# Linear attention: the queries' features as the stationary operand, denominators as a 65th column, the result turned for the output product

## The chip, the cores and the metric

One Trainium2 chip, one of its cores. The metric is the device time of one execution in microseconds (us), the median of several. A core has TensorE (PE; its weight loads are listed as PEld), VectorE (DVE), ScalarE (ACT), GpSimd (POOL) and SyncE (SP), which runs the DMA queue used here. The engines run side by side and order their work by semaphores.

## The reference

Eight sublayers in a row, each added to x (16 batches of 112 rows of 256). The change is in the third, a linear attention of x to a context of 375 rows:

```python
B, L, HID, H, DH, M = (4, 1024, 256, 16, 64, 128)
def _relu_kernel(x, proj):
    ratio = 1.0 / float(np.sqrt(proj.shape[0]))
    return jax.nn.relu(ratio * jnp.einsum('blhd,md->blhm', x, proj)) + EPS
q = jnp.einsum('bld,dhk->blhk', query_input, Wq)
k = jnp.einsum('bld,dhk->blhk', source_input, Wk)
v = jnp.einsum('bld,dhk->blhk', source_input, Wv)
qp = _relu_kernel(q, proj)
kp = _relu_kernel(k, proj)
kvs = jnp.einsum('blhm,blhd->bhmd', kp, v)
num = jnp.einsum('blhm,bhmd->blhd', qp, kvs)
ks_sum = jnp.sum(kp, axis=1)
den = jnp.einsum('blhm,bhm->blh', qp, ks_sum)
att = num / den[..., None]
return jnp.einsum('blhd,hdk->blk', att, Wo)
```

So 16 heads of 64 values, each with 128 features per row.

## The kernel before

The sublayer is `linear_attention_phase`. Most products are made from 16-bit parts: an operand is split into a high half (`HI`, ScalarE as a rule) and a low half (`LO`, VectorE or GpSimd), and a product is the sum of three (`PARTS`).

All engines walk through the same list of steps, 16 to a batch (`SLOTS`), written out by hand in `units_at`. Within a batch, t counts its steps. In steps 0 to 7 a key product is made per step (`k`); the features of the keys (`features`) are made in steps 5, 7, 9, 10, 12 and 14, the values (`v`) in steps 8, 9, 11, 12, 13 and 15. Every second batch also makes the queries of two batches: `q` in the odd steps, their features (`qf`) in steps 6, 10, 14 and 18. A batch then goes on under the steps of the next one: the sums over the context in steps 18 to 21 (`sums`, 36 products of 65 columns each; the 65th column of the values is one, so it holds the sum of the features), then `den`, `ratio` and `out`. Step 16 + n of a batch is step n of the next, and within a step the older batch comes first.

Each engine takes the units of a step in that order, and its queue is strict:

- TensorE makes the products. Those of `k`, `v`, `q`, `features` and `qf` go to five PSUM banks in a ring (`p_bank`); before a bank is written, TensorE waits until the unit that held it has been taken (`claim`, `taken`). Three banks hold the sums (`kvs_bank`), the numerators and the output (`num_bank`) and the broadcast denominators (`den_bank`).
- ScalarE makes the high parts: those of keys, queries and values from PSUM; those of the features one step later, from `kp` (`high_features`).
- VectorE makes the low parts of keys, queries and values, and takes the features from PSUM (ReLU and the small constant) to `kp`, which has four places.
- GpSimd makes the low parts of the features (`low_features`, L1260), two instructions per unit, and those of the divided result (`low_att`, L1266), and splits the next context in step 4.

The quotient before: in step 22 `denominators` (L1566) multiplies the queries' features with the sums of the features, FP32, 16 products into four groups of 32 rows. VectorE (`invert`) takes the reciprocal and splits it in three bfloat16 parts. In steps 25 and 28 `ratio` makes the numerators of eight heads, transposed (64 values x 112 rows, FP32, two heads at a time), and spreads the reciprocals over the rows with 12 bfloat16 products against a selector. ScalarE copies the numerators (`take_num`), VectorE multiplies (`divide`), ScalarE and GpSimd split the result (`high_att`, `low_att`, steps 27 and 30). In step 35 `out_product` (L1596) makes 24 products, and VectorE adds the result to X in step 36.

The context of a batch comes by DMA from SyncE, once GpSimd's split has emptied the buffer.

Of the kernel before, what the change touches and what calls it, by code (L numbers as in the profile page):

```python
# [17 lines left out]
H = 16  # L18
# [1096 lines left out]
def linear_attention_phase(nc, tag, X, XT, ident, ctxT, Wq, Wk, projT, Wv, Wo):  # L1115
# [50 lines left out]
    with ExitStack() as st:  # L1166
# [10 lines left out]
        qp = qp_flat[:, :].rearrange("p (g r c s) -> p g r c s", g=2, r=2, c=C)  # L1177
# [9 lines left out]
        summed, kvs_evac, den_done, inverted, divided, att_done, out_done, x_done = (  # L1187
            m.sem(n) for n in ("summed", "kvs_evac", "den_done", "inverted", "divided", "att_done", "out_done", "x_done"))
        dks_blank, sel_made, num_taken = m.sem("dks_blank"), m.sem("sel_made"), m.sem("num_taken")
        wo_hi, wo_split, att_hi, att_split, part, rden_split = (  # L1190
            m.sem(n) for n in ("wo_hi", "wo_split", "att_hi", "att_split", "part", "rden_split"))
# [38 lines left out]
        kvs = m.sb("kvs", [128, H, VC])  # L1230
        dks = m.sb("dks", [128, H, 32])
        sel = m.sb("sel", [128, C, 128], BF16)
        rden = m.sb("rden", [128, 3, S])
        rden16 = m.sb("rden16", [128, 3, S], BF16)
        wo16 = m.sb("wo16", [128, 2, C, D], F16)
        att16 = m.sb("att16", [128, 2, C, S], F16)
        attT = m.sb("attT", [128, C, S])
        p_bank = [m.bank(f"p{i}") for i in range(RING)]
        kvs_bank, num_bank, den_bank = m.bank("kvs_sum"), m.bank("num"), m.bank("den")

        with nc.Block() as block:
# [7 lines left out]
            def _(pool):  # L1249
# [14 lines left out]
                def low_att(b, hf):  # L1264
                    pool.wait_ge(att_hi, 2 * b + hf + 1)
                    pool.tensor_tensor(att16[:, LO, 4 * hf:4 * hf + 4, :], attT[:, 4 * hf:4 * hf + 4, :],  # L1266
                                       att16[:, HI, 4 * hf:4 * hf + 4, :], ALU.subtract).then_inc(att_split, 1)

                split_context(0)
                pool.memset(dks[:, :, :], 0.0).then_inc(dks_blank, 1)  # L1270
                pool.memset(v16[:, HI, :, :, DH:VC], 1.0).then_inc(ones_made, 1)
                pool.memset(v16[:, LO, :, :, DH:VC], 0.0).then_inc(ones_made, 1)
                for h in range(H):
                    row = 32 * (h % 4) + 8 * (h // 4)
                    pool.tensor_copy(sel[:, h // 2, h % 2 * DH:(h % 2 + 1) * DH],
                                     ident[:, row:row + 1].to_broadcast([128, DH])).then_inc(sel_made, 1)
                for s in steps:
                    for unit in units_at(s):
                        if unit[0] == "features":
                            low_features(unit)  # L1280
                    if s % SLOTS == 4 and s // SLOTS + 1 < B:
                        split_context(s // SLOTS + 1)
                    for b in range(B):
                        if s - SLOTS * b in (27, 30):
                            low_att(b, (s - SLOTS * b - 27) // 3)

            @block.scalar
            def _(act):
# [11 lines left out]
                def evacuate(unit):  # L1300
# [19 lines left out]
                    elif kind == "sums":  # L1320
                        act.wait_ge(summed, 4 * b + c + 1)
                        if b >= 1:
                            act.wait_ge(divided, 2 * b)
                        act.copy(kvs[:, 4 * c:4 * c + 4, :],
                                 src[:, 0:4 * VC].rearrange("p (h d) -> p h d", d=VC)).then_inc(kvs_evac, 1)
                        if b == c == 0:
                            act.wait_ge(dks_blank, 1)
                        if b >= 1:
                            act.wait_ge(den_done, b)
                        act.copy(dks[:, 4 * c:4 * c + 4, 8 * c:8 * c + 8],  # L1330
                                 src[:, 0:4 * VC].rearrange("p (h d) -> p h d", d=VC)[:, :, DH:VC].to_broadcast([128, 4, 8])
                                 ).then_inc(kvs_evac, 1)

                def take_num(b, hf):
                    act.wait_ge(divided, 2 * b + hf + 1)
                    if b >= 1:
                        act.wait_ge(out_done, b)
                    act.copy(attT[:, 4 * hf:4 * hf + 4, :].rearrange("p n s -> p (n s)"), num_bank[:, 0:4 * S]).then_inc(num_taken, 1)

                def high_att(b, hf):  # L1340
                    act.wait_ge(att_done, 2 * b + hf + 1)
                    act.copy(att16[:, HI, 4 * hf:4 * hf + 4, :], attT[:, 4 * hf:4 * hf + 4, :]).then_inc(att_hi, 1)
# [17 lines left out]
                for s in steps:  # L1360
                    if s >= 1:
                        for unit in units_at(s - 1):
                            if unit[0] == "features":
                                high_features(unit)
                    for unit in units_at(s):
                        if unit[0] in ("k", "q", "v", "sums"):
                            evacuate(unit)
                        elif unit[0] == "ratio":
                            take_num(unit[1], unit[2])
# [3 lines left out]
                    for b in range(B):  # L1373
                        if s - SLOTS * b in (27, 30):
                            high_att(b, (s - SLOTS * b - 27) // 3)
# [6 lines left out]
            def _(dve):  # L1382
# [5 lines left out]
                def take(unit):  # L1388
                    kind, b, c = unit
                    bank = place[unit][0]  # L1390
                    src = p_bank[bank]
# [23 lines left out]
                    elif kind == "qf":  # L1415
                        dve.wait_ge(projected["qf"], qfeats[unit] + 1)
                        if b >= 2:
                            dve.wait_ge(divided, 4 * b - 4)
                        for r, bank in enumerate(place[unit]):
                            dve.tensor_scalar(qp[:, b % 2, r, 2 * c:2 * c + 2, :],  # L1420
                                              p_bank[bank][:, 0:2 * QW].rearrange("p (c s) -> p c s", s=QW), 0.0, EPS * WS,
                                              ALU.max, ALU.add).then_inc(qp_done, 1)

                def invert(b):
                    dve.wait_ge(den_done, b + 1)
                    if b >= 1:
                        dve.wait_ge(divided, 2 * b)
                        dve.wait_ge(rden_split, b)
                    dve.reciprocal(rden[:, 0, :], kvs_bank[:, 384:384 + S]).then_inc(inverted, 1)
                    dve.wait_ge(inverted, b + 1)  # L1430
                    for i in range(2):
                        dve.tensor_copy(rden16[:, i, :], rden[:, i, :]).then_inc(part, 1)
                        dve.wait_ge(part, 4 * b + 2 * i + 1)
                        dve.tensor_tensor(rden[:, i + 1, :], rden[:, i, :], rden16[:, i, :], ALU.subtract).then_inc(part, 1)
                        dve.wait_ge(part, 4 * b + 2 * i + 2)
                    dve.tensor_copy(rden16[:, 2, :], rden[:, 2, :]).then_inc(rden_split, 1)

                def divide(b, hf):
                    half = attT[:, 4 * hf:4 * hf + 4, :].rearrange("p n s -> p (n s)")
                    dve.wait_ge(num_taken, 2 * b + hf + 1)  # L1440
                    dve.tensor_tensor(half, den_bank[:, 0:4 * S], half, ALU.mult).then_inc(att_done, 1)
# [5 lines left out]

                dve.wait_ge(wk_hi, 1)
# [1401 lines left out]
```

## Time and profile before

| | |
|---|---|
| time, median of 3 runs | 2585.32 us (2584.45 to 2588.91) |
| the profiled execution | 2593.29 us, of which span 2591.3 us |
| PE busy over the span | 2213.3 us (85%), 23986 products |
| DVE, ACT, POOL busy | 1561.2, 1411.5, 953.2 us |
| mean granted clock of TensorE | 0.92 of full speed |

The phase of the change runs from about 518 us to 1125 us of the span. The time is the median; the rows come from the one profiled execution. In the rows, `a_kp` is a feature tile, `a_p` the ring of banks, `a_kvs_sum`, `a_num` and `a_den` the three other banks; "128*112" behind a product is rows x columns of its stationary operand, followed by the moving one.

### The profile page before, as it was taken

The numbers are of one execution on the slowest core, as the hardware profiler recorded it, in microseconds if no ns is written. First come the engines' busy times: TensorE is split into PE (matmuls) and PEld (weight loads), VectorE is DVE, ScalarE is ACT, GpSimd is POOL, SyncE is SP. The second block draws the span as 40 slices with busy tenths as digits, with TensorE's granted clock in tenths as the row PEclk, the third lists the DMA queues.
The fourth block names the chain that finished last, engine by engine and source line by source line (L and its number), as shares of the span: only waits on it lengthen the run. The fifth ranks groups of instructions, "written<-read, shape, count | busy, mean of one in ns | idle before, by whom it ended". The sixth has DMA issues, their size and how long they took to land. (4 is left out here: it accounts for less than half of the span.)

```text
span 2591.3 us, 62717 instructions
## 1 busy us (share of the span) xinstructions
PE 2213.3 (85%) x23986; PEld 1467.9 (57%) x23986; DVE 1561.2 (60%) x3640; ACT 1411.5 (54%) x2999; POOL 953.2 (37%) x1066
## 2 busy tenths in 40 slices
PE   5889399599999999968699999999974993899755
PEld 2556255367777777745456666666652541566533
DVE  3667572476566556636767777777756544556463
ACT  3666563365555555425466666666663542566543
POOL 3443222154444444404423333333322632433043
PEclk8999699799999999969899999999986995999978
DMA  6563361300000000010200000000023214333133
GB/s 129 111 116 71 111 216 38 119 20 14 14 14 8 14 14 2 2 33 1 87 14 9 15 14 9 15 14 9 2 85 103 67 56 124 87 79 73 26 114 109
DMA packets 118581, 139.59 MB, mean 54 GB/s; under 512 B 15072, under 2 KB 107184, under 8 KB 118288
## 3 DMA queue, kind: packets, MB, share of 16 engines
q1 hardware_dynamic: 110900, 115.39, 17.3%
q0 software_dynamic: 7392, 20.19, 2.5%
q8 instruction: 200, 3.28, 0.5%
q14 instruction: 89, 0.73, 0.1%
HBM read 93.25 MB, written 17.47 MB: 43 GB/s over the span
## 5 line engine op out<-in xcount | busy, mean ns | idle before, releaser
L952 DVE TENSOR_REDUCE a_mx<-a_pair 112x2 f32<-112x750 f32 x256 | 238.0, 936 | 194.9 <-PE a_pair L1021 194.9
L1260 POOL TENSOR_TENSOR a_kp<-a_kp 125x512 f16<-125x512 f32 x192 | 217.6, 1158 | 259.1 <-ACT a_kp L1351 259.1
L353 POOL TENSOR_SCALAR a_P<-a_P,a_inv 112x375 f32<-112x375 f32 x256 | 148.4, 593 | 378.5 <-DVE a_inv L484 377.4
L890 ACT ACTIVATE a_PT<-a_pair 125x672 f32<-125x672 f32 x256 | 186.2, 730 | 71.1 <-PE a_pair L1033 66.3
L391 ACT ACTIVATE a_P<-a_masked,a_least 112x375 f32<-112x375 f32 x256 | 153.5, 600 | 83.5 <-DVE a_least L479 81.6
L1394 DVE SCALAR_TENSOR_TENSOR a_k<-a_p,a_k 128x375 f16<-128x375 f32 x128 | 69.3, 547 | 138.7 <-ACT a_k L1307 138.7
L1351 ACT CAST a_kp<-a_kp 125x512 f16<-125x512 f32 x192 | 110.4, 617 | 76.4 <-DVE a_kp L1413 76.4
L572 PE MATMUL a_p<-a_kc,a_wk 128*128 128x375 f16 x768 | 147.1, 327 | 4.3 <-POOL a_kc L347 4.3
L1493 PE MATMUL a_p<-a_kc,a_wk 128*128 128x375 f16 x768 | 142.4, 327 | 6.3 <-POOL a_kc L1252 6.3
L586 PE MATMUL a_p<-a_wv,a_kc 128*125 128x512 f16 x576 | 141.9, 383 | 5.2 <-DVE a_v L518 3.6
L479 DVE CUSTOM_DVE_ANT_0 a_masked<-a_s,a_mask_add 112x375 f32<-112x375 f32 x256 | 129.9, 545 | 27.1 <-PE a_s L609 26.1
L1493 PE MATMUL a_p<-a_wv,a_kc 128*125 128x512 f16 x576 | 141.0, 385 | 0.0
L2522 ACT ACTIVATE all_XT<-f_hb 128x512 f32<-128x512 f32 (+1 forms) x98 | 53.2, 549 | 152.6 <-PE f_hb L2434 136.2
L2434 PE MATMUL f_hb<-w_w1h,f_x 128*128 x588 | 134.9, 367 | 0.0
L1413 DVE TENSOR_SCALAR a_kp<-a_p 125x512 f32<-125x512 f32 x192 | 122.8, 681 | 8.2 <-PE a_p L1524 8.2
L509 DVE SCALAR_TENSOR_TENSOR a_k<-a_p,a_k 128x375 f16<-128x375 f32 x128 | 70.2, 549 | 82.9 <-ACT a_k L402 82.9
L619 PE MATMUL a_t<-all_ident,a_P 112*125 112x112 f32 x768 | 116.6, 288 | 3.4 <-POOL a_P L353 3.4
L489 DVE TENSOR_TENSOR a_PT<-a_t,a_PT 125x336 f16<-125x336 f32 x256 | 116.8, 498 | 1.5 <-ACT a_PT L427 1.5
L619 PEld LDWEIGHTS a_t<-all_ident,a_P 112*125 112x125 f32 x768 | 93.9, 188 | 38.8 <-issue 34.6
L1033 PE MATMUL a_pair<-a_q,a_k 50*125 50x112 f16 (+1 forms) x1536 | 89.5, 224 | 20.7 <-DMA a_q<-a_mT 13.8
L1052 PE MATMUL a_y<-a_PT,a_values 125*32 125x112 f32 x3072 | 102.7, 268 | 5.1 <-ACT a_PT L890 4.9
L586 PEld LDWEIGHTS a_p<-a_wv,a_kc 128*125 128x125 f16 x576 | 77.8, 137 | 49.7 <-DVE a_k L509 6.8
(446 smaller groups left out, 5324.1 us busy)
## 6 DMA issues: line engine op xcount, KB each, us to landing
a_kc<-in_ctxT SPq DMA_DIRECT2D x64, 375.0 KB, 4.0
a_k<-a_k_parts SPq DMA_DIRECT2D x192, 93.8 KB
w_stage<-in_L_ffn_W SPq DMA_DIRECT2D x32, 512.0 KB
w_stage<-in_L_ffn_ew SPq DMA_DIRECT2D x16, 512.0 KB, 6.9
w_stage<-expert_rows SPq DMA_DIRECT2D x16, 448.0 KB, 8.0
a_v_in_sb<-in_ctx SPq DMA_DIRECT2D x16, 375.0 KB
a_q<-a_q_parts SPq DMA_DIRECT2D x48, 112.0 KB, 3.6
w_stage<-in_L_ffn_W SPq DMA_DIRECT2D x16, 256.0 KB, 3.9
```

The source lines that it names most:

```text
L353: pool.tensor_scalar(P[:, p % 4, r, :], P[:, p % 4, r, :], inv[:, p % 4, r:r + 1], 1.0, ALU.mult, ALU.mult).then_inc(P_done, 1)
L391: act.activation(P[:, p % 4, r, :], masked[:, p % 2, r, :], ACT.Exp, bias=least[:, p % 4, r:r + 1], scale=-1.0, accum_out=total[:, p % 4, ...
L479: dve.tensor_tensor_reduce(masked[:, p % 2, r, :], s_bank[0:S, r, 0:SK], mask_add[:, b % 2, :], 1.0, 3e38, ALU.add, ALU.min, least[:, p % ...
L572: mm = pe.matmul(out[:, 0:SK], wk16[:, z, j, c * 128:(c + 1) * 128], kc16[:, b % 2, x, j, :], start=i == j == 0, stop=(i, j) == (2, DC - 1))
L586: mm = pe.matmul(out[0:KP, 0:512], kc16[:, b % 2, x, j, jk * KP:(jk + 1) * KP], wv16[:, z, j, w * 512:(w + 1) * 512], start=i == j == 0, s ...
L619: mm = pe.transpose(t_bank[0:KP, r, j * S:(j + 1) * S], P[:, p % 4, r, j * KP:(j + 1) * KP], ident[0:S, 0:S])
L890: act.activation(PT[:, p % 4, :, :], pair_bank[slot["turned", p]][0:KP, :, 0:KT * S], ACT.Exp).then_inc(exp_done, 1)
L952: dve.tensor_reduce(mx[:, b % 2, 2 * pair:2 * pair + 2], pair_bank[slot["score", p]][0:S, :, 0:SK], AX.X, ALU.max).then_inc(max_done, 1)
L1260: pool.tensor_tensor(kp16[:, LO, j, hf, r, :, :].rearrange("p c m -> p (c m)"), kp[:, n % 4, :], kp16[:, HI, j, hf, r, :, :].rearrange("p ...
L1413: dve.tensor_scalar(kp[:, n % 4, :], p_bank[bank][0:KP, 0:512], 0.0, EPS * WS, ALU.max, ALU.add).then_inc(f_evac, 1)
L1493: mm = pe.matmul(out, lhs(x, z, j), rhs(x, z, j), start=i == j == 0, stop=(i, j) == (2, DC - 1))
L2434: mm = pe.matmul(bank[:, 0:BW], x16[:, j % 2, x, c, :], w.w1h[:, z, c, bass.ds(e, 1), cols].rearrange("p o f -> p (o f)"), start=False, st ...
```

## The change

The quotient is made the other way round, with the rows of x on the partitions.

- The queries' features are now split in 16-bit parts: VectorE writes them to `qpf` (four places), ScalarE makes the high part one step later (`high_queries`), GpSimd the low part (`low_queries`).
- The sums are split too: ScalarE makes the high part from `kvs_bank`, and VectorE the low part from the same bank after it; TensorE's next sums wait for the latter.
- `denominators`, the reciprocal's parts, the selector and the broadcast are gone. `weigh` in steps 23 and 25 makes, per head, three products with the features of 112 rows as stationary operand and the 65 columns of the head's sums moving: seven heads, then nine. Column 65 is the denominator of each row.
- VectorE divides (`divide`, steps 24 and 26) per row with a reciprocal per head. ScalarE and GpSimd split the result, in steps 26 and 28 (before 27 and 30).
- `turn` in step 31 transposes both parts, eight products each; the high part waits for ScalarE's two halves, the low part for GpSimd's two. ScalarE copies the turned high part (`take_high`) and VectorE the low one (`take_low`) for the output product, which stays in step 35.

```diff
-            found += [("den", b, 0)] if t == 22 else []
-            found += [("ratio", b, 0)] if t == 25 else [("ratio", b, 1)] if t == 28 else []
+            found += [("num", b, 0)] if t == 23 else [("num", b, 1)] if t == 25 else []
+            found += [("turn", b, 0)] if t == 31 else []
...
+        pieces = [[(first_bank, 0, 0, 7)], [(num_bank, 0, 7, 14), (kvs_bank, 4 * VC, 14, 16)]]
+        halves = (slice(0, 7), slice(7, H))
...
+                def low_queries(unit):
+                    _, g, c = unit
+                    for r in range(2):
+                        n = 2 * qfeats[unit] + r
+                        pool.wait_ge(qp_hi, n + 1)
+                        pool.tensor_tensor(qp16[:, g % 2, LO, r, 2 * c:2 * c + 2, :],
+                                           qpf[:, n % 4, :].rearrange("p (c s) -> p c s", s=QW),
+                                           qp16[:, g % 2, HI, r, 2 * c:2 * c + 2, :], ALU.subtract).then_inc(qp_low, 1)
+
+                def low_att(b, i):
+                    pool.wait_ge(att_hi, 2 * b + i + 1)
+                    pool.tensor_tensor(atr16[:, LO, halves[i], :], att[:, halves[i], :], atr16[:, HI, halves[i], :],
+                                       ALU.subtract).then_inc(att_split, 1)
...
-                for h in range(H):
-                    row = 32 * (h % 4) + 8 * (h // 4)
-                    pool.tensor_copy(sel[:, h // 2, h % 2 * DH:(h % 2 + 1) * DH],
-                                     ident[:, row:row + 1].to_broadcast([128, DH])).then_inc(sel_made, 1)
                 for s in steps:
                     for unit in units_at(s):
                         if unit[0] == "features":
                             low_features(unit)
+                        elif unit[0] == "qf":
+                            low_queries(unit)
                     if s % SLOTS == 4 and s // SLOTS + 1 < B:
                         split_context(s // SLOTS + 1)
                     for b in range(B):
-                        if s - SLOTS * b in (27, 30):
-                            low_att(b, (s - SLOTS * b - 27) // 3)
+                        if s - SLOTS * b in (26, 28):
+                            low_att(b, (s - SLOTS * b - 26) // 2)
...
+                        act.mul(kvs16[:, HI, 4 * c:4 * c + 4, :], src[:, 0:4 * VC].rearrange("p (h d) -> p h d", d=VC),
+                                1.0 / WS).then_inc(kvs_hi, 1)
...
+                def take_high(b):
+                    act.wait_ge(att_turned, 2 * b + 1)
+                    if b >= 1:
+                        act.wait_ge(out_done, b)
+                    act.copy(att16[:, HI, :, :].rearrange("p c s -> p (c s)"),
+                             first_bank[:, :].bitcast(F16)[:, 0:C * S]).then_inc(high_taken, 1)
+
+                def high_queries(unit):
+                    _, g, c = unit
+                    if g >= 2:
+                        act.wait_ge(weighed, 4 * g - 4)
+                    for r in range(2):
+                        n = 2 * qfeats[unit] + r
+                        act.wait_ge(qp_done, n + 1)
+                        act.copy(qp16[:, g % 2, HI, r, 2 * c:2 * c + 2, :],
+                                 qpf[:, n % 4, :].rearrange("p (c s) -> p c s", s=QW)).then_inc(qp_hi, 1)
...
+                    else:
+                        dve.wait_ge(kvs_hi, 4 * b + c + 1)
+                        dve.scalar_tensor_tensor(kvs16[:, LO, 4 * c:4 * c + 4, :],
+                                                 kvs_bank[:, 0:4 * VC].rearrange("p (h d) -> p h d", d=VC), 1.0 / WS,
+                                                 kvs16[:, HI, 4 * c:4 * c + 4, :], ALU.mult, ALU.subtract).then_inc(kvs_done, 1)
+
+                def divide(b, i):
+                    dve.wait_ge(weighed, 2 * b + i + 1)
                     if b >= 1:
...
+                        dve.wait_ge(att_split, 2 * b)
+                    for piece in pieces[i]:
+                        h0, h1 = piece[2:]
+                        dve.reciprocal(rden[:, h0:h1].unsqueeze(2), weights_of(*piece)[:, :, DH:VC]).then_inc(inverted, 1)
+                    for n, piece in enumerate(pieces[i]):
+                        h0, h1 = piece[2:]
+                        dve.wait_ge(inverted, 3 * b + i + n + 1)
+                        ins = dve.tensor_tensor(att[:, h0:h1, :], weights_of(*piece)[:, :, 0:DH],
+                                                rden[:, h0:h1].unsqueeze(2).to_broadcast([S, h1 - h0, DH]), ALU.mult)
+                    ins.then_inc(att_done, 1)
...
-                        pe.wait_ge(kvs_evac, 8 * b + 2 * g)
+                        pe.wait_ge(kvs_done, 4 * b + g)
...
+                def weigh(b, i):
                     g, t = divmod(b, QB)
...
+                    pe.wait_ge(kvs_done, 4 * b + 2 * i + 2)
+                    pe.wait_ge(qp_low, 8 * (g + 1))
+                    if b >= 1 and i == 0:
+                        pe.wait_ge(high_taken, b)
+                    elif b >= 1:
                         pe.wait_ge(x_done, b)
...
+                    for piece in pieces[i]:
+                        bank, at, h0, h1 = piece
+                        for h in range(h0, h1):
+                            for n, (x, z) in enumerate(PARTS):
+                                mm = pe.matmul(bank[0:S, at + (h - h0) * VC:at + (h - h0 + 1) * VC],
+                                               qp16[:, g % 2, x, h % 2, h // 2, t * S:(t + 1) * S], kvs16[:, z, h, :],
+                                               start=n == 0, stop=n == 2)
+                    mm.then_inc(weighed, 1)
+
+                def turn(b):
+                    if b == 0:
+                        pe.wait_ge(ready16, 1)
+                    for x, bank, made in ((HI, first_bank, att_hi), (LO, num_bank, att_split)):
+                        pe.wait_ge(made, 2 * b + 2)
+                        for c in range(C):
+                            mm = pe.transpose(bank[:, :].bitcast(F16)[:, c * S:(c + 1) * S],
+                                              atr16[:, x, 2 * c:2 * c + 2, :].rearrange("s h d -> s (h d)"), ident16[:, :])
+                        mm.then_inc(att_turned, 1)
+
                 def out_product(b):
-                    pe.wait_ge(att_split, 2 * b + 2)
+                    pe.wait_ge(high_taken, b + 1)
+                    pe.wait_ge(low_taken, b + 1)
```

## Rows read from the trace of the kernel before

**Rows 1.** Windows, 35 us of the phase: busy us per engine, granted clock, DMA, GB/s.

```profile
878.00:913.00 35.00, 34.67 (x508) 26.50 (x506) 22.05 (x44) 18.03 (x41) 14.51 (x13) 1.00 0.04 13
```

**Rows 2.** Timeline of PE, batch without queries: start, length, engine, line, product, count.

```profile
847.64 1.26 PE L1554 MATMUL a_kvs_sum<-a_v,a_kp 125*128 125x65 f16 x36
848.73 1.13 PE L1493 MATMUL a_p<-a_kc,a_wk 128*128 128x375 f16 x6
849.70 1.25 PE L1554 MATMUL a_kvs_sum<-a_v,a_kp 125*128 125x65 f16 x36
...
854.73 0.97 PE L1566 MATMUL a_kvs_sum<-a_qp,a_dks 128*32 128x112 f32 x32
855.64 2.10 PE L1493 MATMUL a_p<-a_kc,a_wk 128*128 128x375 f16 x12
...
860.08 0.99 PE L1582 MATMUL a_num<-a_qp,a_kvs 128*64 128x112 f32 x16
861.00 0.76 PE L1586 MATMUL a_den<-a_rden,a_sel 128*128 128x112 bf16 x12
861.70 0.91 PE L1524 MATMUL a_p<-a_pp,a_k 64*125 64x128 f16 x24
862.53 1.51 PE L1493 MATMUL a_p<-a_wv,a_kc 128*125 128x512 f16 x6
...
872.27 1.51 PE L1493 MATMUL a_p<-a_wv,a_kc 128*125 128x512 f16 x6
```

**Rows 3.** Timeline of PE in another sublayer, 112 stationary columns, 120 to 8 moving.

```profile
305.32 1.52 PE L2482 MATMUL f_o<-f_hot,r_ones 112*112 112x120 f16 x15
306.70 0.23 PE L2484 MATMUL f_o<-f_heads,r_ones 112*112 112x8 f16 x1
```

**Rows 4.** Windows over those products (columns as in rows 1).

```profile
305.00:310.00 5.00, 1.74 (x17) 1.68 (x17) 4.66 (x15) 2.99 (x5) 0.00 (x0) 0.50 0.40 125
```

**Rows 5.** Groups by line, 518 to 1130 us: count, busy us, mean ns, idle before.

```profile
L1260 POOL TENSOR_TENSOR a_kp<-a_kp 125x512 f16<-125x512 f32 x192 | 217.6, 1158 | 259.1 <-ACT a_kp L1351 259.1
...
L1266 POOL TENSOR_TENSOR a_att<-a_attT,a_att 128x448 f16<-128x448 f32 x32 | 33.1, 1036 | 21.2 <-ACT a_att L1342 21.2
...
L1324 ACT COPY a_kvs<-a_kvs_sum 128x260 f32<-128x260 f32 x64 | 24.0, 375 | 72.2 <-PE a_kvs_sum L1554 72.2
...
L1441 DVE TENSOR_TENSOR a_attT<-a_den,a_attT 128x448 f32<-128x448 f32 x32 | 19.7, 615 | 7.2 <-ACT a_attT L1338 7.2
```

**Rows 6.** Timeline of POOL, low parts of steps 9 and 10, both kinds of batch.

```profile
828.10 4.51 POOL L1260 TENSOR_TENSOR a_kp<-a_kp 125x512 f16<-125x512 f32 x4 [1.59 <-ACT a_kp L1351]
...
865.26 4.51 POOL L1260 TENSOR_TENSOR a_kp<-a_kp 125x512 f16<-125x512 f32 x4 [1.12 <-ACT a_kp L1351]
```

**Rows 7.** Timeline of PE, values of steps 9 and 15, batch with queries.

```profile
825.04 1.51 PE L1493 MATMUL a_p<-a_wv,a_kc 128*125 128x512 f16 x6
...
838.33 1.51 PE L1493 MATMUL a_p<-a_wv,a_kc 128*125 128x512 f16 x6
```

**Rows 8.** Timeline of the phase's end, with idle time before in brackets.

```profile
1091.57 1.51 PE L1493 MATMUL a_p<-a_wv,a_kc 128*125 128x512 f16 x6
...
1097.08 4.33 PE L1596 MATMUL a_num<-a_wo,a_att 128*112 128x256 f16 x24 [2.92 <-POOL a_att L1266]
...
1103.15 1.25 PE L1554 MATMUL a_kvs_sum<-a_v,a_kp 125*128 125x65 f16 x36 [0.65 <-ACT a_dks L1330]
...
1124.84 0.42 DVE L1445 SCALAR_TENSOR_TENSOR all_X<-a_num,all_X 112x256 f32<-112x256 f32 x1 [6.29 <-PE a_num L1596]
```

**Rows 9.** Windows of 1 us: the clock comes back (columns as in rows 1).

```profile
144.00:145.00 1.00, 1.00 (x22) 0.69 (x14) 0.77 (x3) 0.39 (x1) 0.00 (x0) 0.76 1.08 159
...
1100.00:1101.00 1.00, 1.00 (x10) 1.00 (x9) 0.00 (x0) 0.00 (x0) 0.00 (x0) 0.90 0.00 0
```

**Rows 10.** Timeline of PE, a group of six after idle times in another sublayer.

```profile
80.64 0.38 PE L1033 MATMUL a_pair<-a_q,a_k 50*125 50x112 f16 x6 [2.09 <-DMA a_q<-a_mT]
...
139.15 0.57 PE L1033 MATMUL a_pair<-a_q,a_k 50*125 50x112 f16 x6 [3.25 <-DMA a_q<-a_mT]
```

More of the change, by code:

```diff
@@ L1322, in evacuate @@
                         if b >= 1:
[L1323 to L1332, printed above, removed]
@@ L1389, in take @@
                     kind, b, c = unit
-                    bank = place[unit][0]
-                    src = p_bank[bank]
+                    src = kvs_bank if kind == "sums" else p_bank[place[unit][0]]
                     if kind == "k":
@@ L1424, in invert @@
-                def invert(b):
-                    dve.wait_ge(den_done, b + 1)
-                    if b >= 1:
[L1427 to L1441, printed above, removed]
+                            n = 2 * qfeats[unit] + r
+                            if n >= 4:
+                                dve.wait_ge(qp_low, n - 3)
+                            dve.tensor_scalar(qpf[:, n % 4, :], p_bank[bank][:, 0:2 * QW], 0.0, EPS * WS, ALU.max,
+                                              ALU.add).then_inc(qp_done, 1)
+                    else:
[3 more added lines that the diff above has]
+                                                 kvs16[:, HI, 4 * c:4 * c + 4, :], ALU.mult, ALU.subtract).then_inc(kvs_done, 1)
@@ L1462, in _ @@
                     for unit in units_at(s):
-                        if unit[0] in ("k", "q", "v", "features", "qf"):
+                        if unit[0] in ("k", "q", "v", "features", "qf", "sums"):
                             take(unit)
@@ L1557, in sums @@
                     mm.then_inc(summed, 1)
-                def denominators(b):
+                def weigh(b, i):
                     g, t = divmod(b, QB)
-                    pe.wait_ge(kvs_evac, 8 * b + 8)
-                    taken(pe, ("qf", g, 3), 1)
-                    for i in range(H // 4):
-                        for a in range(4):
-                            h = 4 * i + a
-                            mm = pe.matmul(kvs_bank[32 * a:32 * a + 32, 384:384 + S], dks[:, h, :],
-                                           qp[:, g % 2, h % 2, h // 2, t * S:(t + 1) * S], start=i == 0, stop=i == H // 4 - 1)
-                    mm.then_inc(den_done, 1)
@@ L1604, in _ @@
                             sums(unit[1], unit[2])
-                        elif unit[0] == "den":
-                            denominators(unit[1])
-                        elif unit[0] == "ratio":
-                            ratio(unit[1], unit[2])
+                        elif unit[0] == "num":
+                            weigh(unit[1], unit[2])
+                        elif unit[0] == "turn":
+                            turn(unit[1])
                         elif unit[0] == "out":
```

94 lines of the change are left out of this document (38 added, 56 removed).

## The prediction

> **What bounds the kernel now.** I read the 35 us windows of the phase first. The reader is to see that TensorE is busy for all but a third of a microsecond at full clock, while VectorE, ScalarE and GpSimd are busy for 22, 18 and 15 us [rows 1]. So in the linear attention (518 to 1125 us of the span) a microsecond taken from TensorE's queue is a microsecond of the kernel, and each wait of TensorE that is added costs its whole length. Second, the timeline of TensorE gives the price of each group from start to start [rows 2, 7]. Third, GpSimd's timeline and groups show how far behind TensorE the low parts come [rows 5, 6]. Last, the end of the phase and the clock after idle stretches [rows 8 to 10].
>
> **TensorE's work per batch.** Removed: denominators, 854.73 to 855.64 = 0.91 us, and twice a ratio, 860.08 to 861.70 = 1.62 us [rows 2]; together 4.15 us. Added: 16 heads x 3 = 48 products, with 112 columns stationary and 65 moving, and 16 turning products. No row shows 112x65. The sums (128 stationary, 65 moving) take 847.64 to 848.73 for 36, 30 ns each [rows 2]. The nearest row with 112 stationary columns has 15 products with 120 down to 8 moving columns, in 305.32 to 306.70, 92 ns each [rows 3], at a granted clock of 0.50 [rows 4]; their moving columns average 64, which at 1.2 GHz would be 53 ns, while 112 columns are 93 ns: the stationary part sets their pace, and at full clock that is 46 ns. Bounds for the 48: 1.45 us and 2.2 us. I take 2.2, since that row has this number of stationary columns.
>
> The Trainium skill (TensorE: Matmul & The Clock Gate, section Weight-path perf modes) says that the fast weight load is on only when the number of weights is 128 and the type is not FP32. By that rule the 112 columns load slowly, as the row at half clock has it, and the sum is 2.2 us; if they loaded as the sums' 128 do it would be 1.45.
>
> The turning products have 128 stationary and 112 moving 16-bit columns, like the 12 broadcasts at 861.00 to 861.70, 58 ns each [rows 2]: 16 x 58 ns = 0.93 us, 0.46 for either part. TensorE saves 4.15 - 2.2 - 0.93 = 1.0 us per batch (1.8 by the other bound).
>
> **The wait that is added.** The turning product of batch b stands in step 31, which is step 15 of the next batch, and needs GpSimd's second low part of the divided rows. GpSimd issues that in step 28 (step 12 of the next batch) behind the low parts of the features of steps 9, 10 and 12 and behind its own first half; in batches with queries also behind two low parts of query features (step 10). Before, the output product of step 35 was what waited for it, four steps later. Worked out from the end of the features of step 9, which is the start of the values' product of step 9:
> - Batch without queries. TensorE: 862.53 to 872.27 = 9.74 us, less the second ratio that has moved or gone, 1.62, plus the high half of the turning, 0.46: it wants the low part at 8.6 us [rows 2]. GpSimd: starts 865.26, that is 2.7 us in, 4.5 us for four feature parts [rows 6], 1.04 for 448 elements, 2.3 for two feature parts, and for 576 elements (by the step from 448 to 512) 1.3 [rows 5]: 11.9 us. TensorE waits 3.3 us.
> - Batch with queries. TensorE: 825.04 to 838.33 = 13.3, less 1.62 plus 0.46 = 12.1 us [rows 7]. GpSimd: starts 828.10, so 3.1 + 4.5 + two query parts of 448 elements, 2.1, + 1.0 + 2.3 + 1.3 = 14.3 us [rows 5, 6]. It waits 2.1 us, part of it perhaps sooner, where the query product of step 14 claims a bank.
>
> Behind the waiting turn stand the values' product of step 15 and then everything; nothing else on TensorE can go ahead, so the wait is lost. The turns fall in batches 1 to 15, of which 8 are without queries and 7 with: 8 x (3.3 - 1.0) + 7 x (2.1 - 1.0) = 26 us more.
>
> **The clock.** After 3.25 us without a product TensorE went on at half clock [rows 10], until 144.5, 5.3 us later (0.76 in that microsecond [rows 9]); after 2.92 us [rows 8] until 1100.2, 3.1 us later [rows 9]. After 2.09 us a group of six still took 0.38 us, not 0.57 [rows 10]. So I expect the 3.3 us waits to cost the clock and the 2.1 us waits not to. TensorE's queue is full after them, so half of the slow stretch is lost: 1.6 to 2.6, say 2.1 us, x 8 = 17 us.
>
> **Sums.** The next sums waited for ScalarE alone (copy 0.375 us [rows 5], done just before one key product had passed). Now VectorE reads the same bank after it; 260 elements by the 0.615 us for 448 [rows 5] are about 0.42 us. Sums end + 0.2 + 0.38 + 0.05 + 0.42 = 1.05 to 1.1 us against the key product's 0.97 (848.73 to 849.70): 0.1 us, some 1.5 times per batch, 3 us in all.
>
> **Costed at nothing.** VectorE loses the inversion and its five small operations and gains four low parts of the sums, three small reciprocals and the 896-element copy; ScalarE gains four query parts per batch and loses eight small copies. Each gains 1 to 1.5 us per batch beside 13 and 17 us idle [rows 1]. If that cover were gone it would be TensorE's banks that come back late, at most those 1.5 us per batch, 24 us. GpSimd's sixteen selector copies at the start go too; nothing waits for them before the first ratio. The small copy of the identity ahead of VectorE's first split adds 0.2 us. No transfer is added or moved: the context's loads still wait for GpSimd's split in step 4.
>
> **The end.** Before: from the last values' product to the last add 1091.57 to 1125.26, 33.7 us [rows 8]. There the output product waited 2.92 us for GpSimd, then ran at half clock; the chain of the inversion and two halves, one after the other, followed. After, counted from the same product (estimates from the rows above): values and the copies out of the turn 3.8; output product 2.6 at full clock; three sums, now 2.2 apart instead of 1.25 + 0.65 = 1.9 [rows 8], 5.5; weighing 2.5; dividing 1.4; high part 0.7; low part 1.3; low turn at half clock and its copy 2.0; output 4.5 and add 0.4: 25 us. That gives back 9 us.
>
> **Sum.** +26 + 17 + 3 + 0.2 - 9 = +37 us. On the profiled execution, 2591.3 us of span and 2.0 around it, that makes 2630. That execution stood 0.3% above the median of the runs; on the median, 2585.3, it makes 2622.
>
> **Rivals.**
> - *The wait without the clock.* For it: the waits could come out a few tenths shorter, and one gap of 2.09 us left the clock alone. Against it: gaps of 2.92 and 3.25 us both lost it. +20 us: 2605.
> - *No wait at all: faster.* GpSimd's low part would have to be ready 3.3 us sooner relative to TensorE, for instance if its parts of features came 1 us each rather than 1.16 and ScalarE's high parts sooner. Then 16 x 1.0 us and the 9 us of the end come in, less 3 for the sums: -22 us, 2563; with 30 ns for a weighing product, -12 more. It decides where the wait falls under 1.0 us in a batch. Against it: its busy time and start are rows, and between features 9 and the turn GpSimd has no idle time to give.
> - *A wait of half the size,* since TensorE's earlier arrival at the features lets ScalarE and GpSimd begin sooner: about 1.2 us per batch. 15 x (1.2 - 1.0) + 3 - 9 = -3 us, within 0.2%: 2582.
> - *More waits.* The 2.1 us waits lose the clock too (7 x 2.1 = 15 us), or ScalarE's extra parts delay the features: 2637, at most 2660.
> - *The change does less than it says:* were 16-bit weighing as dear as FP32, TensorE would save nothing: 16 us on the forecast, 2638.
>
> **Chances.** Forecast 0.46, wait without the clock 0.20, half wait 0.08, faster 0.14, the two dear ones 0.12. Range: left out are the faster case and most of what lies above 2650, so 2590 to 2650. The slower cases' own range is 2600 to 2650. Within 0.2% (5 us, about what a measurement of this kernel can tell from no change): 0.08; faster 0.14; slower 0.78.
>
> **What the profile after would show.** Right: a row of idle time before the low half of the turning product, released by GpSimd's low part of the divided rows, about 3 us in batches without queries and 2 in the others; granted clock under 1.00 in the windows of the batches without queries; weighing products 46 ns apart; about 1 us less matmul work per batch at full clock; the last output product some 9 us closer to the last values. Wrong: GpSimd idle ahead of that low part, windows at 1.00 throughout, or waits of TensorE elsewhere (banks, sums). The likeliest ways to be wrong are the length of the wait, a difference of two long sums, and how long the clock stays down.

## The result, and the profile after

The changed kernel takes 2624.49 us (median of 4 runs, 2622.21 to 2634.08), the kernel before, run beside it, 2585.91. The ratio is 1.0155, 95% interval 1.0127 to 1.0182: slower by about 1.5%, 38.6 us between the medians. The forecast was 2622, that is +37.

The profiled execution of the changed kernel is the longest of its four, 2634.08 us, and some 6 us of that lie ahead of the phase: its first key product starts at 524.31 us, against 518.13 before. So I measure the phase by itself, from that product to the end of the last add. Before: 518.13 to 1125.26, 607.1 us. After: 524.31 to 1169.92, 645.6 us, 38.5 more. That is as much as the medians differ by. The agreement is closer than it can be relied on: a second execution of the changed kernel, below, has a phase of 640.8 us, and the phase before is known from one execution only, which lies 8 us above its median.

Windows over the same 35 us of the span as [rows 1], changed kernel (length, then busy us of PE, PEld, DVE, ACT, POOL with counts, granted clock, DMA share, GB/s):

```profile
878.00:913.00 35.00, 31.82 (x428) 23.35 (x423) 19.18 (x38) 17.27 (x35) 19.31 (x17) 0.95 0.05 13
```

TensorE was busy for 34.67 us at full clock in [rows 1]; now 3.2 us are empty, the clock is down for a part, and 80 products fewer are done. GpSimd has gained 4.8 us of work. The timeline of TensorE shows the place, first a batch without queries, then one with queries, then the sums (start, length, engine, line, product, count; in brackets idle time and its releaser):

```profile
826.73 0.57 PE L1609 MATMUL a_first<-a_ident,a_atr 112*128 112x112 f16 x8
830.36 0.93 PE L1609 MATMUL a_num<-a_ident,a_atr 112*128 112x112 f16 x8 [3.06 <-POOL a_atr L1281]
...
868.01 0.91 PE L1551 MATMUL a_p<-a_pp,a_k 64*125 64x128 f16 x24
869.77 0.75 PE L1561 MATMUL a_p<-a_q,a_pp 64*128 64x224 f16 x12 [0.85 <-DVE a_v L1422]
870.45 0.57 PE L1609 MATMUL a_first<-a_ident,a_atr 112*128 112x112 f16 x8
872.26 0.57 PE L1609 MATMUL a_num<-a_ident,a_atr 112*128 112x112 f16 x8 [1.24 <-POOL a_atr L1281]
872.66 1.47 PE L1520 MATMUL a_p<-a_wv,a_kc 128*125 128x512 f16 x6
...
1120.79 1.13 PE L1520 MATMUL a_p<-a_kc,a_wk 128*128 128x375 f16 x6
1121.98 1.25 PE L1581 MATMUL a_kvs_sum<-a_v,a_kp 125*128 125x65 f16 x36
```

The low half of the turn waits for GpSimd's low part in every one of the 15 batches that turn beside a following one: about 3.05 us in the 8 without queries, 1.24 us in the 7 with queries. In those 7 the query product of step 14 also waits 0.85 us for its bank (0.28 us in the kernel before). The sums that have only a key product ahead of them start 1.19 us after it, where [rows 2] have 0.97; there are three such places in two batches.

The bank wait grew from 0.28 to 0.85 us because of ScalarE's queue. Here is ScalarE, first in the changed kernel, then in the kernel before:

```profile
866.24 0.60 ACT L1330 ACTIVATE a_v<-a_p 125x512 f16<-125x512 f32 x1 [1.28 <-PE a_p L1520]
866.74 0.66 ACT L1343 CAST a_atr<-a_att 112x576 f16<-112x576 f32 x1
867.30 1.14 ACT L1369 CAST a_kp<-a_kp 125x512 f16<-125x512 f32 x2
868.34 0.60 ACT L1330 ACTIVATE a_v<-a_p 125x512 f16<-125x512 f32 x1
```

```profile
835.19 1.13 ACT L1351 CAST a_kp<-a_kp 125x512 f16<-125x512 f32 x2
836.22 0.60 ACT L1318 ACTIVATE a_v<-a_p 125x512 f16<-125x512 f32 x1
...
836.95 0.57 ACT L1342 CAST a_att<-a_attT 128x448 f16<-128x448 f32 x1
```

The second high part of the divided rows moved from step 30 to step 28. It now stands ahead of the features and of the values' high part, where it stood behind them. Counted from TensorE's values' product of steps 12 and 13 (864.70 now, 833.15 before), the values' high part starts after 3.64 us instead of 3.07. VectorE's low part, which gives the bank back, comes after it. These 0.57 us are the growth of the wait; the piece was not moved back to try it.

The weighing products, in the timeline of the batch that begins at 800.85:

```profile
811.99 1.23 PE L1598 MATMUL a_first<-a_kvs,a_qp 128*112 128x65 f16 x21
813.05 1.13 PE L1520 MATMUL a_p<-a_kc,a_wk 128*128 128x375 f16 x6
...
816.29 1.23 PE L1598 MATMUL a_num<-a_kvs,a_qp 128*112 128x65 f16 x21
817.36 0.48 PE L1598 MATMUL a_kvs_sum<-a_kvs,a_qp 128*112 128x65 f16 x6
817.77 0.91 PE L1551 MATMUL a_p<-a_pp,a_k 64*125 64x128 f16 x24
```

21 products take 811.99 to 813.05 = 1.06 us, 50.5 ns each; both groups together 1.06 + 1.48 = 2.54 us per batch. A half of the turn takes 872.26 to 872.66, 0.40 us, 50 ns for each of 8.

The clock after one of the long waits, in windows of 1 us (columns as above):

```profile
829.00:830.00 1.00, 0.00 (x0) 0.00 (x0) 0.31 (x1) 0.96 (x2) 1.00 (x2) 1.00 0.00 0
830.00:831.00 1.00, 0.65 (x8) 0.65 (x9) 0.00 (x0) 0.00 (x0) 1.00 (x2) 0.56 0.00 0
831.00:832.00 1.00, 1.00 (x7) 0.61 (x5) 0.00 (x0) 0.00 (x0) 1.00 (x2) 0.50 0.00 0
832.00:833.00 1.00, 1.00 (x4) 0.61 (x3) 0.00 (x0) 0.00 (x0) 0.52 (x1) 0.50 0.00 0
833.00:834.00 1.00, 1.00 (x6) 0.45 (x5) 0.00 (x0) 0.20 (x1) 0.00 (x0) 0.73 0.00 0
834.00:835.00 1.00, 1.00 (x8) 0.61 (x7) 0.57 (x1) 1.00 (x2) 0.00 (x0) 1.00 0.00 0
```

In this turn the granted clock is still 1.00 for most of the idle time, falls to 0.50 (1.2 GHz of 2.4) in the last quarter of a microsecond before the low half starts, and stays there for 0.44 x 2 + 2 + 0.27 x 2 = 3.4 us. In other turns the fall comes later, up to 1.0 us after the low half has started (the first, at 590.17). Between 560 us and the tail such stretches sum to 37.5 us, as much as eleven of 3.4 us: one at each of the 8 long waits, of which that at 670 us lasts 6.8, and one each near 632 and 714 us, at turns that had waited 1.24 us. The kernel before has none there before 1096 us.

This fall costs about 1.5 us: the low half of the turn takes 0.72 us (830.36 to 831.08) and not 0.40, the values' product behind it 2.52 us (831.08 to 833.60) and not 1.34.

GpSimd's timeline in the last batch, and its groups by line and shape over the phase (count, busy us, mean ns, idle before):

```profile
1135.27 4.50 POOL L1266 TENSOR_TENSOR a_kp<-a_kp 125x512 f16<-125x512 f32 x4 [2.40 <-ACT a_kp L1369]
1139.73 1.04 POOL L1281 TENSOR_TENSOR a_atr<-a_att,a_atr 112x448 f16<-112x448 f32 x1
1140.73 2.27 POOL L1266 TENSOR_TENSOR a_kp<-a_kp 125x512 f16<-125x512 f32 x2
1142.95 1.28 POOL L1281 TENSOR_TENSOR a_atr<-a_att,a_atr 112x576 f16<-112x576 f32 x1
```

```profile
L1275 POOL TENSOR_TENSOR a_qp<-a_qpf,a_qp 128x448 f16<-128x448 f32 x64 | 66.0, 1052 | 41.1 <-ACT a_qp L1359 41.1
...
L1444 DVE SCALAR_TENSOR_TENSOR a_kvs<-a_kvs_sum,a_kvs 128x260 f16<-128x260 f32 x64 | 27.4, 428 | 72.4 <-ACT a_kvs L1336 72.2
L1336 ACT ACTIVATE a_kvs<-a_kvs_sum 128x260 f16<-128x260 f32 x64 | 24.8, 387 | 68.3 <-PE a_kvs_sum L1581 68.3
```

GpSimd has no idle time between the low parts of step 9 and the one that TensorE waits for: 1144.23 - 1135.27 = 8.96 us in one piece. The 64 new query parts add 66 us to its phase.

The tail, in the timeline of all engines, answers to [rows 8]:

```profile
1144.29 0.93 PE L1609 MATMUL a_num<-a_ident,a_atr 112*128 112x112 f16 x8 [3.05 <-POOL a_atr L1281]
...
1145.01 2.73 PE L1520 MATMUL a_p<-a_wv,a_kc 128*125 128x512 f16 x6
...
1154.70 1.25 PE L1581 MATMUL a_kvs_sum<-a_v,a_kp 125*128 125x65 f16 x36 [1.03 <-DVE a_kvs L1444]
...
1165.35 4.11 PE L1620 MATMUL a_num<-a_wo,a_att 128*112 128x256 f16 x24 [0.81 <-DVE a_att L1466]
...
1169.50 0.42 DVE L1471 SCALAR_TENSOR_TENSOR all_X<-a_num,all_X 112x256 f32<-112x256 f32 x1 [4.30 <-PE a_num L1620]
```

From the last values' product to the last add it is now 24.9 us, where [rows 8] have 33.7.

### The profile page after: what moved, and what is told of

It is laid out like the page before. It is cut to its first block and busy times, and to the rows that moved or that the text cites. A ratio compares the mean times of both kernels' runs of the same rounds, so it can differ in the third digit from the quotient of the medians.

```text
span 2632.4 us, 62104 instructions
## 1 busy us (share of the span) xinstructions
PE 2226.3 (85%) x23602; PEld 1477.7 (56%) x23602; DVE 1575.7 (60%) x3689; ACT 1438.1 (55%) x2983; POOL 1014.8 (39%) x1113
## 5 line engine op out<-in xcount | busy, mean ns | idle before, releaser
L1520 PE MATMUL a_p<-a_wv,a_kc 128*125 128x512 f16 x576 | 152.5, 409 | 0.0
L586 PE MATMUL a_p<-a_wv,a_kc 128*125 128x512 f16 x576 | 141.9, 383 | 5.2 <-DVE a_v L518 3.6
L1422 DVE SCALAR_TENSOR_TENSOR a_v<-a_p,a_v 125x512 f16<-125x512 f32 x96 | 66.5, 693 | 112.4 <-ACT a_v L1330 112.4
L1330 ACT ACTIVATE a_v<-a_p 125x512 f16<-125x512 f32 x96 | 57.3, 597 | 101.4 <-PE a_p L1520 101.4
```

The costliest lines, as they stand in the source:

```text
L586: mm = pe.matmul(out[0:KP, 0:512], kc16[:, b % 2, x, j, jk * KP:(jk + 1) * KP], wv16[:, z, j, w * 512:(w + 1) * 512], start=i == j == 0, s ...
L1520: mm = pe.matmul(out, lhs(x, z, j), rhs(x, z, j), start=i == j == 0, stop=(i, j) == (2, DC - 1))
```

## The experiments

Theory: the loss is the turn's place in TensorE's queue, ahead of GpSimd's low part, and the clock that goes with the wait; the arithmetic itself is cheaper. Rivals: the clock alone, or the slow 112-column weighing, or the sums' new wait carries it. The kernels ran on two other chips, with the kernel before beside each set: its median was 2582.85 us for the first four (19 runs) and 2596.41 us for the second four (9 runs). So ratios are compared, and phases of profiled executions, each measured as above. The phases are of one execution each, and no execution of the kernel before was profiled on these two chips.

**Turn two steps later.** The turn and the two copies that take it move from step 31 to step 33:

```diff
-            found += [("turn", b, 0)] if t == 31 else []
+            found += [("turn", b, 0)] if t == 33 else []
```

(and the same number in ScalarE's and VectorE's lists). 

> The changed kernel, with the turning product and its two copies moved from step 31 to step 33; nothing else. Theory (the turning product waits for GpSimd's second low part, and the clock falls after the long waits): both waits (8 x 3.15 us and 7 x 1.4 us, 35 us in all) and the clock's loss (17 us) go, 2624.5 - 52 = about 2572 us, granted clock 1.00 through the phase, faster than the kernel before. Rival A (the wait only moves on, to the output product of step 35, which needs the copies): 2600 or more, with an idle stretch before the output product. Rival B (the time is lost in banks that VectorE and ScalarE give back late under their extra work): 2615 to 2625, the waits of TensorE for VectorE grown.

Measured: 2582.01 us, ratio 0.9999 (0.9985 to 1.0014); phase 599.8 us. Timeline of TensorE, batch without queries:

```profile
727.54 0.56 PE L1609 MATMUL a_first<-a_ident,a_atr 112*128 112x112 f16 x8
728.86 0.57 PE L1609 MATMUL a_num<-a_ident,a_atr 112*128 112x112 f16 x8 [0.76 <-POOL a_atr L1281]
```

The whole loss is gone, and the clock is at full until the tail (behind the phase's first microseconds, which are at half clock in every profile). But I had expected 10 us less. The wait did not vanish in the batches without queries, it is 0.77 us (1.72 in the last of them); and two batches, from output product to output product, take 73.26 us, as in the kernel before (73.10). What the products save there, the rest of this wait, the bank wait of step 14 and the sums use up. In the profiled execution only the shorter end is left as a gain (7.3 us of phase). That execution is 6 us below this kernel's own median; the median gains 0.8 us, and where the other 6 go is not settled. It had the highest mean granted clock of the ten executions (0.921; the median is 0.916, and the slowest, 2588.49 us, had 0.912), so the clock may be where they go, in a part of the kernel that no kept trace shows.

**Low part first on GpSimd.** The turn stays; GpSimd makes the second low part in step 27, ahead of the features of step 12:

```diff
-                        if s - SLOTS * b in (26, 28):
-                            low_att(b, (s - SLOTS * b - 26) // 2)
+                        if s - SLOTS * b in (26, 27):
+                            low_att(b, s - SLOTS * b - 26)
```

> The changed kernel, with GpSimd's second low part of the divided rows issued at the end of step 27, so ahead of the low parts of the features of step 12 instead of behind them; the turning product stays in step 31. Theory (GpSimd's queue makes the part late): the wait shrinks by the two feature parts, 2.3 us: 3.15 to 0.9 us in batches without queries, 1.4 to 0 in the others, and with 0.9 us the clock stays up: 2624.5 - 28 - 17 = about 2579 us. Rival (the part is late because VectorE's division and ScalarE's high part are, and the place in GpSimd's queue is no matter): the wait stays near 3 us, 2624 us.

Measured: 2578.50 us, ratio 0.9982 (0.9967 to 0.9997); phase 601.0 us. TensorE in a batch without queries:

```profile
728.01 0.57 PE L1609 MATMUL a_first<-a_ident,a_atr 112*128 112x112 f16 x8
729.40 0.57 PE L1609 MATMUL a_num<-a_ident,a_atr 112*128 112x112 f16 x8 [0.82 <-POOL a_atr L1281]
```

3.05 became 0.82 us, as two feature parts of 1.16 us less would have it; in batches with queries the wait is gone. So where one instruction stands in the queue of GpSimd, which is idle for 16 of 35 us, decides between 1.0155 and 0.9982.

**The same wait, filled.** TensorE repeats the high half of the turn while it waits, 8 times in batches without queries and 4 times in the others; the repeats write the same values again:

```diff
-                        for c in range(C):
+                        again = (8 if b % 2 == 0 else 4) if x == HI and b < B - 1 else 1
+                        for c in list(range(C)) * again:
```

> The changed kernel, but TensorE repeats the eight products that turn the high part while it would wait: 8 times over in batches without queries, 4 times in the others (8 products take 0.41 us), into the same place. The added products compute nothing new. Theory (the wait itself is 35 us, the clock's fall after it is a further cost of about 17 us): idle stretches of 0.3 and 0.2 us are left, the granted clock stays at 1.00, and the time falls by 14 to 18 us, to about 2609 us. Rival (half clock costs nothing here, since what follows waits for others anyway, or the clock falls in spite of the fill): 2624 us or a little more.

Measured: 2605.86 us, ratio 1.0095 (1.0073 to 1.0117); phase 630.2 us. TensorE:

```profile
738.62 3.32 PE L1610 MATMUL a_first<-a_ident,a_atr 112*128 112x112 f16 x64
742.25 0.57 PE L1610 MATMUL a_num<-a_ident,a_atr 112*128 112x112 f16 x8 [0.31 <-POOL a_atr L1281]
742.65 1.47 PE L1520 MATMUL a_p<-a_wv,a_kc 128*125 128x512 f16 x6
```

The turn ends as late as ever, TensorE only stays busy. The clock is at full until the tail, and the phase is 15.4 us shorter than the changed kernel's; the ratio says 0.6%, 16 us. This is the price of the clock by itself. It is known roughly: against the second execution of the changed kernel, below, the phase is 10.6 us shorter, but the ratio 0.7% lower, 18 us. The rival that the clock alone made the change slow falls too: 1.0095 is left, which is the wait.

**128 stationary columns.** The query features of each batch are stored 128 apart instead of 112, the 16 added columns zero, and the weighing products use all 128:

```diff
-                                mm = pe.matmul(bank[0:S, at + (h - h0) * VC:at + (h - h0 + 1) * VC],
-                                               qp16[:, g % 2, x, h % 2, h // 2, t * S:(t + 1) * S], kvs16[:, z, h, :],
+                                mm = pe.matmul(bank[:, at + (h - h0) * VC:at + (h - h0 + 1) * VC],
+                                               qp16[:, g % 2, x, h % 2, h // 2, t, :], kvs16[:, z, h, :],
```

> The changed kernel, but the queries' features are stored 128 columns apart with 16 blank columns behind each batch's 112, and the weighing products take all 128 as stationary operand (their 16 extra result rows are not read). Theory (the 112 stationary columns set the pace of 51 to 53 ns for 65 moving columns, 128 load faster): 30 ns a product as in the sums, 48 x 21 ns = 1.0 us per batch, 16 us in all: about 2608 us. Rival (the pace is set by the moving part and the issue of the instructions): 50 ns a product as before, 2624 us.

Measured: 2613.17 us, ratio 1.0121 (1.0099 to 1.0144); phase 634.5 us. TensorE:

```profile
720.13 0.81 PE L1604 MATMUL a_first<-a_kvs,a_qp 128*128 128x65 f16 x21
720.77 1.12 PE L1524 MATMUL a_p<-a_kc,a_wk 128*128 128x375 f16 x6
```

More columns are faster: 21 products in 0.64 us, 30.5 ns each against 50.5; 1.57 us per batch against 2.54, so 15.5 us in 16 batches. The Trainium skill (TensorE: Matmul & The Clock Gate, section Weight-path perf modes) has fast weight load on only for 128 weights that are not FP32; by that rule the trace agrees. The edit also moves the places of the features in memory; that and the number of columns were not tried apart. With 1.0121 left, the slow weighing is not what made the change slow. Only 11 us of the 15.5 show in the phase. The clock accounts for most of the rest: half-clock stretches sum to 44.4 us up to the tail instead of 37.5, at 7 of the 8 long waits and now at 5 of the 7 short ones; 6.9 / 2 = 3.4 us of work lost, as an estimate. Two turns of this one execution, both of batches with queries:

```profile
776.09 0.75 PE L1565 MATMUL a_p<-a_q,a_pp 64*128 64x224 f16 x12 [0.85 <-DVE a_v L1426]
...
778.56 0.57 PE L1615 MATMUL a_num<-a_ident,a_atr 112*128 112x112 f16 x8 [1.23 <-POOL a_atr L1282]
778.97 2.73 PE L1524 MATMUL a_p<-a_wv,a_kc 128*125 128x512 f16 x6
...
854.38 0.75 PE L1565 MATMUL a_p<-a_q,a_pp 64*128 64x224 f16 x12 [0.85 <-DVE a_v L1426]
...
856.86 0.57 PE L1615 MATMUL a_num<-a_ident,a_atr 112*128 112x112 f16 x8 [1.23 <-POOL a_atr L1282]
857.27 1.47 PE L1524 MATMUL a_p<-a_wv,a_kc 128*125 128x512 f16 x6
```

The waits are the same, 0.85 and 1.23 us, and the values' product after them takes 2.73 us once and 1.47 us the other time.

**The changed kernel again,** on the second chip, as the measure for the next three. 

> The changed kernel once more, unaltered, beside the kernel before on the chip of the runs it is sent with: 1.5% slower again (1.013 to 1.018), the phase 38 us longer. It is there to be compared with.

Measured: 2638.39 us, ratio 1.0165 (1.0149 to 1.0181); phase 640.8 us. The clock fell 8 times up to the tail, after the long waits alone. So the two further falls of the first profile and the long one at 670 us come and go between executions (here on two chips); they are three times 3.4 us, and the phases differ by 645.6 - 640.8 = 4.8 us.

**Two banks for the sums.** The four groups of sums alternate between `kvs_bank` and `first_bank`:

```diff
+        sum_bank = (kvs_bank, first_bank)
...
-                    if 4 * b + g >= 1:
-                        pe.wait_ge(kvs_done, 4 * b + g)
+                    if 4 * b + g >= 2:
+                        pe.wait_ge(kvs_done, 4 * b + g - 1)
+                    if b >= 1 and g == 1:
+                        pe.wait_ge(high_taken, b)
```

> The changed kernel, but every second group of sums goes to the bank that is free until the weighing, so the next sums need not wait for VectorE's low part of the last (the weighing then waits for all four low parts). Theory (between one sums and the next in the same bank a key product of 0.97 us covers all but 0.22 us of the two readers, three times in two batches; in the end 1.03 us twice): 8 x 0.66 + 2 = about 7 us less than the changed kernel, the turn's waits and the clock as they were. Rival (the gap is TensorE's own, between two kinds of product): no difference. Beside it: TensorE arrives earlier nowhere between the features of step 9 and the turn, so the waits there keep their length.

Measured: 2635.53 us, ratio 1.0145 (1.0126 to 1.0165); phase 641.3 us. The sums follow their key products after 0.97 us again. So the longer gap was VectorE's part and not TensorE's own. The gain of 7 us that was expected is not shown: the phase of the profiled execution gains nothing, and the intervals of the two ratios overlap. In this execution the clock fell at 4 of the 7 short waits too, and at none in the control: 44.4 us at half clock up to the tail against 27.3, which at 1.5 us for each 3.4 is 7.5 us, as much as the banks should have brought. So the gain may be there and covered; that is argued, not shown. The next sums are not all that changed: the weighing now waits for all four low parts.

**The later turn with 128 columns.** Both edits above. 

> The changed kernel with the turning product in step 33 and the 128-column stationary operand. Theory (the two costs are separate and TensorE is the bound again once the turn's wait is nearly gone): the phase 15.5 us shorter than with step 33 alone (599.8 us), 584 us, so 23 us under the kernel before in the phase: about 0.991 of its time. Rival (with less work on TensorE, VectorE or ScalarE or GpSimd become the bound): 592 us or more.

Measured: 2576.57 us, ratio 0.9933 (0.9914 to 0.9951); phase 585.5 us. Where the clock stays up, the wide products bring nearly their whole price: 599.8 - 585.5 = 14.3 us of 15.5, between profiles of two chips.

**All four edits.** Turn in step 33, low part first, 128 columns, two banks. 

> The changed kernel with all four: turn in step 33, GpSimd's second low part ahead of the features of step 12, 128 columns stationary, sums in alternating banks. Theory: 584 us less the last wait before the low half of the turn (8 x 0.77 = 6 us) less 7 us for the sums: about 571 us, 36 us under the kernel before in the phase, 0.986 of its time. What is left over then is the wait of the query product of step 14 (0.85 us in every second batch). Rival (the four overlap, because the other engines' queues now hold TensorE back): 580 us or more, with the banks' waits grown.

Measured: 2563.24 us, ratio 0.9878 (0.9857 to 0.9900), so 1.2% faster than the kernel before; phase 571.8 us. TensorE in a batch without queries, and what is left in one with:

```profile
719.67 0.56 PE L1618 MATMUL a_first<-a_ident,a_atr 112*128 112x112 f16 x8
720.07 0.56 PE L1618 MATMUL a_num<-a_ident,a_atr 112*128 112x112 f16 x8
...
754.46 0.75 PE L1566 MATMUL a_p<-a_q,a_pp 64*128 64x224 f16 x12 [0.85 <-DVE a_v L1427]
```

No turn waits until the tail. Two batches take 69.72 us (output products at 692.90 and 762.62) against 73.10. The 0.85 us at the bank of step 14 is the last idle time of TensorE in the pattern; its removal was not tried. The high part that ScalarE makes ahead of the values still stands in step 28 here, as in all these kernels.

## Why the prediction was right

- **The wait.** Its place, its cause and its two sizes were as worked out: 3.3 us predicted without queries, 3.05 shown as idle (3.63 us from the high half to the low half, less the 0.40 of the products: 3.2); 2.1 us with queries, 1.41 by the same count and 0.57 more at the query product of step 14, together 1.98 (14.3 - 12.1 is 2.2, not 2.1, but it changes nothing). The wait at the query product has a cause of its own, ScalarE's high part in its new place; it costs nothing here, because TensorE would only have waited the longer for GpSimd. GpSimd's low part came 11.7 us after the end of the features of step 9 (1132.55 to 1144.23), predicted 11.9. The first two experiments, which change nothing but who comes first, show it as the cause.
- **TensorE's saving.** 1.0 us per batch predicted. The weighing took 2.54 us instead of 2.2, since a product takes 50.5 ns, not the 46 that I scaled from half clock, and its groups end with a few tens of ns each. The turn took 0.80 instead of 0.93. 4.15 - 2.54 - 0.80 = 0.8 us. With the waits that is 8 x 3.2 + 7 x 1.98 - 15 x 0.8 = 27.5 us, predicted 26.
- **The clock.** Predicted 8 falls and 17 us. Shown: 27 to 37.5 us at half clock, that is 8 to 11 times 3.4, each at 1.5 us instead of 2.1, so 12 to 17 us; the filled wait gives 11 to 18. The count was low and the price of one high; that the two made up for each other was luck. That the short waits would leave the clock alone held in one execution of the changed kernel and not in the other. This was the rival "more waits" in a small part, 5 us.
- **The sums.** 0.22 us each and not 0.1, three times in two batches, 5 us and not 3: VectorE's part takes 0.43 us and starts only when ScalarE's 0.39 us are over, and the bank is free 1.19 us after the key product began.
- **The end.** 25 us predicted, 24.9 measured: -9.
- **The sum** by measured terms, for the first profile: 27.5 + 16.5 (eleven times 1.5) + 5 - 9 = 40 us, against 38.5 in the phase. The two profiled executions of the changed kernel differ by 4.8 us in the phase, so a forecast within 3 us of the median was in part luck.
- **Costed at nothing.** VectorE and ScalarE still idle for 16 and 18 of 35 us, as the prediction has it, and in this kernel what they gained costs nothing more. But its reason, that busy time beside idle time is cover, is not enough: it counted how much work ScalarE gained and not where the work stands. The high part that moved holds a bank back by 0.57 us in every second batch. This is hidden behind the turn's wait in the changed kernel and comes out when that wait is gone, 7 x 0.57 = 4 us.

Of the rivals, "no wait: faster" was priced at 2563, 22 us under the kernel before. That was too much: with the turn moved, the nearest case, the phase is 7.3 us shorter. Left over are 8 x 0.77 = 6 us of the wait and 4 us at the bank, TensorE saves 0.8 us per batch and not 1.0 (3 us), and the sums cost 5 us and not 3. The kernel with all four edits does come to 2563.24 us, but on another chip (by its ratio it would be 2554 beside 2585.91) and with two gains more, the wide products and the banks, so that this number agrees is chance.

## What to carry to other kernels

When a product is placed in a strict queue by hand, work out from the rows when the slowest engine's input will be there, counting all that this engine does first; an engine that is idle half of the time can still be late by 3 us, and putting its urgent piece ahead of the rest cost nothing here. The same holds for a piece that moves earlier: ScalarE's, put ahead of the values, held a bank back by 0.57 us. A wait of 3 us on TensorE here cost half as much again in clock, so look at the granted clock behind each new wait. Where a stationary 16-bit operand is narrower than 128 columns and few columns move, try padding it; it was tried here with 112 stationary and 65 moving columns.

## What the runs showed that I had not expected

- With 65 moving columns, 112 stationary columns cost 50.5 ns per product and 128 cost 30.5. The bound of 30 ns stood in the prediction; that padding would reach it did not.
- The clock fell after waits of 0.85 and 1.24 us close together, in some turns and not in others with the same waits of the same execution. Over the four kernels that kept the turn and the waits (the changed one, the control, 128 columns, two banks) it fell at 11 of 28 such turns and at 31 of the 32 with a wait of 3.05 us. What decides it stays open.
- Products that only keep TensorE busy were worth about 15 us (11 to 18): the same turn, at the same time, cost less when the wait before it was filled.
- The longer wait at the query product's bank came from ScalarE's queue, though it is VectorE that gives the bank back.
- VectorE's copy of 896 16-bit elements from PSUM took 615 ns, ScalarE's of the same size 900 ns.
